# Down projection by seven products of quarters, with its sums on GpSimd and the next unit's first gate step placed among them

## Time and profile before

| | us |
|---|---|
| median of 3 runs | 4031.17 (4030.34 to 4031.83) |
| profiled execution | 4027.15 |
| its span | 4025.4 |
| feed-forward stage, first to last down product | 104 to 1058 |

### The profile page before, as it was taken

The page is one execution under the profiler, slowest core; times in us unless marked ns, Lnnn a source line. Parts: engine busy times, 40 slices in busy tenths (PEclk is TensorE's granted clock), DMA queues, the critical chain, the costliest instruction groups (busy, mean ns, idle before and its releaser), DMA issues. The chain is left out here.

```text
span 4025.4 us, 83987 instructions
## 1 busy us (share of the span) xinstructions
PE 3942.0 (98%) x29304; PEld 3015.1 (75%) x29304; DVE 3097.8 (77%) x6628; ACT 2298.9 (57%) x5920; POOL 1500.1 (37%) x1881
## 2 busy tenths in 40 slices
PE   7999999999999999999999999999999999999998
PEld 6788787887677777777777776777777777777775
DVE  6666666666588888888888887887888888887885
ACT  2222222222377777667677766767776767677674
POOL 2332232322233333333333334334444444444444
PEclk9999999999999999999999999999999999999999
DMA  4212111120443435344344454444444445445443
GB/s 151 49 37 50 25 50 38 38 50 19 146 113 96 102 100 132 98 104 103 104 106 102 106 143 127 107 132 119 123 115 122 116 120 131 132 116 134 121 109 97
DMA packets 813542, 400.79 MB, mean 100 GB/s; under 512 B 475584, under 2 KB 738752, under 8 KB 813120
## 3 DMA queue, kind: packets, MB, share of 16 engines
q1 hardware_dynamic: 777024, 340.17, 32.4%
q10 hardware_dynamic: 36096, 55.24, 5.0%
HBM read 242.57 MB, written 152.63 MB: 98 GB/s over the span
## 5 line engine op out<-in xcount | busy, mean ns | idle before, releaser
L1250 PE MATMUL bank<-xtile,wt 128*128 128x259 f32 x4096 | 1077.1, 391 | 6.5 <-PEq L766 2.5
L1250 PEld LDWEIGHTS bank<-xtile,wt 128*128 128x128 f32 x4096 | 727.2, 191 | 136.1 <-issue 43.7
L1732 ACT ACTIVATE xyinv<-bank 128x512 f16<-128x512 f32 x768 | 449.9, 590 | 222.0 <-PE bank L1675 217.9
L1989 PE MATMUL bank<-wot,xnt 128*128 128x512 f32 x1024 | 530.9, 610 | 4.0 <-DMA xnt<-x_scratch 3.2
L1708 DVE TENSOR_TENSOR wlev<-bank,mask 128x256 f16<-128x256 f32 x768 | 315.9, 415 | 164.1 <-PE bank L1675 161.1
L1379 DVE SCALAR_TENSOR_TENSOR vraw<-bank,taps,vraw 128x256 f32<-128x256 f32 x768 | 361.1, 476 | 33.8 <-ACT vraw L1372 19.9
L550 PE MATMUL bank<-hb,wt 128*128 128x128 f32 x2816 | 375.5, 277 | 8.3 <-DVE part L590 5.7
L550 PEld LDWEIGHTS bank<-hb,wt 128*128 128x128 f32 x2816 | 349.4, 194 | 17.6 <-issue 7.2
L1675 PEld LDWEIGHTS bank<-xyinv,lth 128*128 128x128 f16 x3584 | 202.6, 98 | 166.4 <-issue 88.3
L613 POOL TENSOR_TENSOR hid<-part 128x256 f32<-128x256 f32 x176 | 139.4, 792 | 473.3 <-ACT part L605 473.3
L1639 POOL TENSOR_TENSOR ltl<-ltm,lth 128x512 f16<-128x512 f32 x128 | 155.7, 1216 | 416.4 <-ACT lth L1633 416.4
(11 more groups left out here) (233 smaller groups left out, 8845.5 us busy)
## 6 DMA issues: line engine op xcount, KB each, us to landing
v_scratch<-vraw SPq DMA_DIRECT2D x64, 512.0 KB, 3.2
vtok<-v_scratch SPq DMA_DIRECT2D x512, 64.0 KB, 2.2
x_scratch<-tq SPq DMA_DIRECT2D x508, 64.0 KB, 1.8
xnt<-x_scratch SPq DMA_DIRECT2D x508, 64.0 KB, 2.5
grows<-row_scratch ACTq DMA_DIRECT2D x126, 256.0 KB, 3.7
k_scratch<-kraw SPq DMA_DIRECT2D x32, 512.0 KB, 2.7
ktok<-k_scratch SPq DMA_DIRECT2D x256, 64.0 KB, 2.1
b_scratch<-kraw SPq DMA_DIRECT2D x256, 64.0 KB, 1.8
```

Source lines behind the costliest of these rows:

```text
L1250: j = pe.matmul(b_p[:, 0:WIN], wt[:, k, c:c + P], xtile[:, par, k, :], **st)
L1732: act.activation(dst, b_inv[p][:].rearrange("p (a h b s) -> p a h b s", a=2, h=HEADS, s=z), ACT.Copy).then_inc(s[f"xy_sb{p}"], 1)
L1989: i = pe.matmul(b_o[:], xnt[:, h], wot[:, h], start=(h == 0), stop=(h == GV - 1))
```

## The change

The down projection becomes seven products too. Features 0 to 4 and 5 to 9 and the two halves of the 512 columns give the blocks d11, d12, d21, d22 of `w_down`; the same features and the two halves of the tokens give c11, c12, c21, c22 of `hid`. Feature block 10 is left over, and its four quarter products are added to four of the seven. POOL makes the weight sums e1, e2, e4 (new tiles) and e3 (in place of d12) once, in steps 0 to 2 (`pool_down_weights`, at "tokens" of unit 0, "stats" and "router" of unit 1). It makes the row sums r1 and r3 after each hid 5 to 9 (`pool_down_rows`), and r2, r4 and `last` in `pool_down`; r2 and r3 and r4 lie in place of c11, c21 and c12. The seven parts down 0 to 6 use 256 columns of banks 6 and 7. Bank 6 gathers sums over down 0, 2, 4, 5; ACT copies it after down 0, 2 and 4, times `routed` (`act_down`), POOL adds rows of h (`dsum`), and DVE selects four quarters (`dve_down`).

In `order`, down 0 and 1 stand where down 0 stood, down 2 to 6 where down 1 stood, and gate step 0 of the next unit is moved ahead of down 5. `dsum`, `last` and `wba` now lie in the end of `wt`, so the load of the z weights moves behind the last store. Some semaphores are merged; a negation of `neg_a` (L676) becomes part of another operation.

```diff
+        FH = FT // 2
+        DOWN = 7
+        lo, hi = slice(0, D // 2), slice(D // 2, D)
+        left, right = slice(0, P), slice(P, 2 * P)
+        d11, d12, d21, d22 = (wd_sb[:, i * FH:(i + 1) * FH, c] for i in range(2) for c in (lo, hi))
+        e3, (e1, e2, e4) = d12, (sb(f"wd_t{i}", [P, FH, D // 2]) for i in (1, 2, 4))
+        c11, c12, c21, c22 = (hid[:, i * FH:(i + 1) * FH, t] for t in (left, right) for i in range(2))
+        r1d, r2d, r3d, r4d = sb("down_s1", [P, FH, P]), c11, c21, c12
+        beyond = both[:, 2 * KT * FF:]
+        dsum = beyond[:, 0:3 * D // 2].rearrange("p (i c) -> p i c", i=3)
+        last = beyond[:, 3 * D // 2:3 * D // 2 + P]
+        DS_W, DS_U = 4, 17
+        DS_S1, DS_S3, DS_S2A, DS_S2, DS_A, DS_LAST, DS_S4, DS_U2, DS_U3 = 9, 10, 11, 12, 13, 14, 15, 16, 17
...
+        def pool_down_weights(pool, step):
+
+            if step == 0:
+                pool.wait_ge(s["d_in"], 16)
+                pool.tensor_tensor(e1[:], d12, d11, ALU.subtract).then_inc(s["dn_pool"], 1)
+                pool.wait_ge(s["dn_pool"], 1)
+                pool.tensor_tensor(e2[:], d22, e1[:], ALU.subtract).then_inc(s["dn_pool"], 1)
+            elif step == 1:
+                pool.wait_ge(s["dn_pool"], 2)
+                pool.tensor_tensor(e4[:], d21, e2[:], ALU.subtract).then_inc(s["dn_pool"], 1)
+            else:
+                pool.tensor_tensor(e3, d22, d12, ALU.subtract).then_inc(s["dn_pool"], 1)
+
+        def pool_down_rows(pool, u, f):
+
+            i = f - FH
+            pool.wait_ge(s["hid_sb"], FT * u + f + 1)
+            pool.tensor_tensor(r1d[:, i], c21[:, i], c22[:, i], ALU.add).then_inc(s["dn_pool"], 1)
+            pool.wait_ge(s["dn_pool"], DS_W + DS_U * u + 2 * i + 1)
+            pool.tensor_tensor(r3d[:, i], c11[:, i], c21[:, i], ALU.subtract).then_inc(s["dn_pool"], 1)
+
+        def pool_down(pool, u, i):
+
+            at, rows, take = DS_W + DS_U * u, h[:, u % 2], pool.tensor_tensor
+            if i == 0:
+                pool.wait_ge(s["d_ps"], DOWN * u + 1)
+                pool.wait_ge(s["dn_pool"], at + DS_S3)
+                for part_of in (slice(0, 2), slice(2, FH)):
+                    take(r2d[:, part_of], r1d[:, part_of], c11[:, part_of], ALU.subtract).then_inc(s["dn_pool"], 1)
+                pool.wait_ge(s["dn_act"], 3 * u + 1)
+                pool.wait_ge(s["hk"], 2 * NJ * (u + 1))
+                take(dsum[:, 0], dsum[:, 0], rows[:, 0, lo], ALU.add).then_inc(s["dn_pool"], 1)
+                pool.wait_ge(s["hid_sb"], FT * (u + 1))
+                take(last, hid[:, FT - 1, left], hid[:, FT - 1, right], ALU.subtract).then_inc(s["dn_pool"], 1)
+            elif i == 1:
+                pool.wait_ge(s["d_ps"], DOWN * u + 2)
+                pool.wait_ge(s["dn_pool"], at + DS_S2)
+                take(r4d, c12, r2d, ALU.subtract).then_inc(s["dn_pool"], 1)
+            elif i == 2:
+                pool.wait_ge(s["dn_act"], 3 * u + 2)
+                take(dsum[:, 1], dsum[:, 1], rows[:, 0, hi], ALU.add).then_inc(s["dn_pool"], 1)
+            elif i == 4:
+                pool.wait_ge(s["dn_act"], 3 * u + 3)
+                take(dsum[:, 2], dsum[:, 2], rows[:, 1, hi], ALU.add).then_inc(s["dn_pool"], 1)
+
+        def pe_down(pe, u, i):
+
+            at, sums = DS_W + DS_U * u, bank[6][:, lo]
+            outs, w10 = bank[7][:, lo], wd_sb[:, FT - 1]
+
+            def product(dst, rows, w, start, stop=True):
+                for f in range(FH):
+                    ins = pe.matmul(dst, rows[:, f], w[:, f], start=start and f == 0, stop=stop and f == FH - 1, skip_group_check=True)
+                return ins
+
+            if i == 0:
+                if u == 0:
+                    pe.wait_ge(s["d_in"], 16)
+                else:
+                    pe.wait_ge(s["selw"], 4 * u - 1)
                 pe.wait_ge(s["h_sb"], added(min(u + 2, UNITS_F)))
-            for f in range(FT):
-                if j == 0:
-                    pe.wait_ge(s["hid_sb"], FT * u + f + 1)
-                i = pe.matmul(bank[6 + j % 2][:], hid[:, f, j * P:(j + 1) * P], wd_sb[:, f, :], start=(f == 0), stop=(f == FT - 1))
-            i.then_inc(s["d_ps"], 1)
-
-        def dve_select(dve, u, j):
-            n = NJ * u + j
-            if n >= 2:
-                dve.wait_ge(s[f"g_out{j % 2}"], 16 * (n // 2))
-            dve.wait_ge(s["hk"], 2 * n + 2)
-            dve.wait_ge(s["d_ps"], n + 1)
-            dve.scalar_tensor_tensor(out=sel[:, j % 2, :], in0=bank[6 + j % 2][:], scalar=routed[:, u % 3, j:j + 1], in1=h[:, u % 2, j, :],
-                                     op0=ALU.mult, op1=ALU.add).then_inc(s["selw"], 1)
-
-        def act_select(act, u, j):
-            act.wait_ge(s["selw"], NJ * u + j + 1)
-            act.activation(sel[:, j % 2, :], sel[:, j % 2, :], ACT.Silu).then_inc(s["g_done"], 1)
+                pe.wait_ge(s["hid_sb"], FT * u + FH)
+                ins = product(sums, c11, d11, True)
+            elif i == 1:
+                if u:
+                    pe.wait_ge(s["selw"], 4 * u)
+                pe.wait_ge(s["hid_sb"], FT * u + 2 * FH)
+                product(outs, c12, d21, True, False)
+                pe.wait_ge(s["hid_sb"], FT * (u + 1))
+                ins = pe.matmul(outs, hid[:, FT - 1, left], w10[:, lo], start=False, stop=True, skip_group_check=True)
+            elif i == 2:
+                pe.wait_ge(s["dn_act"], 3 * u + 1)
+                pe.wait_ge(s["dn_pool"], at + DS_S2A)
+                for f in range(FH):
+                    if f == 2:
+                        pe.wait_ge(s["dn_pool"], at + DS_S2)
+                    ins = pe.matmul(sums, r2d[:, f], e2[:, f], start=False, stop=f == FH - 1, skip_group_check=True)
+            elif i == 3:
+                pe.wait_ge(s["selw"], 4 * u + 1)
+                product(outs, r1d, e1, True, False)
+                ins = pe.matmul(outs, hid[:, FT - 1, right], w10[:, hi], start=False, stop=True, skip_group_check=True)
+            elif i == 4:
+                pe.wait_ge(s["dn_act"], 3 * u + 2)
+                if u == 0:
+                    pe.wait_ge(s["dn_pool"], DS_W)
+                ins = product(sums, r3d, e3, False)
+            elif i == 5:
+                pe.wait_ge(s["dn_act"], 3 * u + 3)
+                product(sums, c22, e4, False, False)
+                ins = pe.matmul(sums, hid[:, FT - 1, right], w10[:, lo], start=False, stop=True, skip_group_check=True)
+            else:
+                pe.wait_ge(s["selw"], 4 * u + 2)
+                pe.wait_ge(s["dn_pool"], at + DS_S4)
+                product(outs, r4d, d22, False, False)
+                ins = pe.matmul(outs, last, w10[:, hi], start=False, stop=True, skip_group_check=True)
+            ins.then_inc(s["d_ps"], 1)
+
+        def act_down(act, u, i):
+
+            if i == 0 and u:
+                act.wait_ge(s["selw"], 4 * u)
+            act.wait_ge(s["d_ps"], DOWN * u + i + 1)
+            scale = routed[:, u % 3, i // 4:i // 4 + 1]
+            act.activation(dsum[:, i // 2], bank[6][:, lo], ACT.Identity, scale=scale).then_inc(s["dn_act"], 1)
+
+        def dve_down(dve, u, i):
+
+            at = DS_W + DS_U * u
+
+            def select(j, half, src, rest):
+                dve.scalar_tensor_tensor(out=sel[:, j, half], in0=src, scalar=routed[:, u % 3, j:j + 1], in1=rest, op0=ALU.mult, op1=ALU.add).then_inc(s["selw"], 1)
+
+            if i == 1:
+                if u:
+                    dve.wait_ge(s["g_out0"], 16 * u)
+                dve.wait_ge(s["dn_pool"], at + DS_A)
+                dve.wait_ge(s["d_ps"], DOWN * u + 2)
+                select(0, lo, bank[7][:, lo], dsum[:, 0])
+            elif i == 4:
+                if u:
+                    dve.wait_ge(s["g_out1"], 16 * u)
+                dve.wait_ge(s["dn_pool"], at + DS_U3)
+                dve.wait_ge(s["d_ps"], DOWN * u + 4)
+                select(1, hi, bank[7][:, lo], dsum[:, 2])
+            elif i == 5:
+                dve.wait_ge(s["hk"], 2 * NJ * (u + 1))
+                dve.wait_ge(s["d_ps"], DOWN * u + 6)
+                select(1, lo, bank[6][:, lo], h[:, u % 2, 1, lo])
+            elif i == 6:
+                dve.wait_ge(s["dn_pool"], at + DS_U2)
+                dve.wait_ge(s["d_ps"], DOWN * u + 7)
+                select(0, hi, bank[7][:, lo], dsum[:, 1])
+
+        def act_select(act, u, i):
+            act.wait_ge(s["selw"], 4 * u + i - 2)
+            act.activation(sel[:, 6 - i, :], sel[:, 6 - i, :], ACT.Silu).then_inc(s["g_done"], 1)
...
-            order.append((("down", 0), u - 1))
+            order += [(("down", i), u - 1) for i in range(2)]
             if u + 1 < UNITS_F:
                 order += [(("normalise",), u + 1), (("router",), u + 1)]
-            order.append((("down", 1), u - 1))
+            order += [(("down", i), u - 1) for i in range(2, DOWN)]
+        for u in range(1, UNITS_F):
+            order.remove((("gate", 0), u))
+            order.insert(order.index((("down", 5), u - 1)), (("gate", 0), u))
...
```

(61 more changed lines are left out.)

9 lines of the change are left out of this document (1 added, 8 removed).

## The result

| us | before | after |
|---|---|---|
| median (4 runs each) | 4031.44 (4030.34 to 4031.83) | 4151.98 (4142.79 to 4155.75) |
| profiled execution | 4027.15 | 4155.75 |
| its first attention product | 1060.35 | 1180.54 |

The ratio is 1.0293 (95% interval 1.0281 to 1.0304): slower by 120.5 us by the medians, forecast 112. The profiled executions differ by 128.6: 120.2 until the first attention product, 8.4 behind it. The one of after is the longest of its four.

What follows compares the result with a forecast made beforehand. PE was taken to bound the kernel, always busy in the feed-forward stage. -32.7 (products) + 91.7 + 10.2 + 2.1 + 0.9 (waits) + 38.5 (clock) + 1 (engines slowing each other) = +111.7, giving 4143 us; range 4096 to 4178.

Steps and rivals of the forecast that it cites:

- The products: PE's down projection: 78 records of 0.216 us replace 44 of 0.429, saving 2.04 us a unit, 32.7 over 16 units.
- The wait: Before down 2, PE waits 7.05 us for r2d, queued on POOL behind the variance step, in 14 of 16 units.
- behind the same keep steps: Remark in the rival that the saving arrives (4000 us, chance 0.03): down 3's select also stands behind DVE's keep steps.
- The clock: After each of 14 long waits PE returns at half rate, losing 2.75 us each, 38.5 in all.
- The rival without the clock: PE waits before down 2 but returns at 2.4 GHz: sum +73.2, 4104 us, chance 0.13.
- The sign given for it: Granted clock goes to 0.50 after each long wait; mean clock of the span falls from 0.994 to about 0.985.
- 1 us for the whole, bounds 0 and 4: Cost of POOL and DVE slowing each other while POOL makes the four weight sums (2.9 us each) at the start.
- The last unit but one: Without the variance step there, down 3 waits for DVE's select and starts at t = 9.0, not 6.91: 2.1 us.
- Against: DVE is idle in just that stretch: Argument against port contention: DVE stands idle while POOL makes r2d and dsum.
- a rival (4158): Port contention: r2d and dsum at 1.45 times their price add 15 us in all, 4158 us, chance 0.09.
- The loads: The z weights' 2 MB load leaves after the last g store, around 1060: taken as 0, upper bound 5 us.
- The moved gate step: Before down 5, it covers ACT's second copy of bank 6, which would otherwise cost PE 0.86 us.

Runs made afterwards that it cites:

- e3: No run: a weight sum POOL makes. The experiment moving e3 and e4 behind down 2's work of the first unit, on the rewritten list: 4004.4 us, ratio 0.9926.
- the rewritten list: Changed kernel with all engines' order rewritten, softplus, keep and statistics steps going between the down parts: 3998.24 us, ratio 0.9925 against the kernel before.
- the first experiment: Changed kernel with only POOL's variance of the next-but-one unit moved behind its work for down 1: 4136.6 us, ratio 1.0266 against the kernel before.
- the one with unused products: Changed kernel with 16 unread products of 256 columns on PE ahead of down 2 in 14 units: 4122.79 us, ratio 1.0229 against the kernel before.
- the one with POOL held back: Changed kernel where, in the last unit but one, POOL's down work waits until DVE has done its softplus parts: one execution, 4152.87 us.

## Why the prediction was right, and where its sizes were off

Slower was right, by the mechanism named and in its range. Profile against profile, by stretches of the sum:

| part | forecast | measured |
|---|---|---|
| start until the first down product | +1 | +5.5 |
| first unit | +10.9 | +11.2 |
| 13 units | 13 x 7.76 = +100.9 | 13 x 7.58 = +98.5 |
| last unit but one | +0.1 | +5.9 |
| last unit | -1.1 | -1.0 |
| attention stage | 0 | +8.4 |

**The products.** -2.04 a unit was exact, as the rewritten list shows where nothing hides it.

**The wait.** 7.05 forecast, 7.27 measured, both from t = 4.75, where down 1 ends by the pace of its records (the waits list counts from the modelled end of the last record and has 7.10). The 0.2 is DVE, slowed in its softplus parts beside POOL's row sums. That it is the list and not POOL's price is shown by taking the operations out of the way (ratio 0.9925). That moving POOL's variance alone would not do is a second thing that the forecast had only as a remark (down 3's select "behind the same keep steps").

**The clock.** 2.75 forecast. From unit to unit down 2 to 6, with the moved gate step among them, take 15.65, 16.6 or 17.1 us in turn instead of 14.03: 1.6 to 3.1, mean 2.4. Keeping PE busy gives 2.28 back. The rival without the clock (4104) is out. That one earlier gap of 5.6 us gave a figure so near the mean is partly luck, as the price differs by a factor of two from wait to wait. The sign given for it, a mean clock near 0.985, was missed: it is 0.977. The granted clock falls while PE still waits (0.74 over 400.20 to 407.20), and so in the feed-forward stage it is at half for 146.8 us, 17.1 before; what of it lies in the wait costs nothing. The Trainium skill, TensorE: Matmul & The Clock Gate, section HAM oscillation, says that a wait which returns in each tile sends the engine to half rate each time; the traces agree, 14 waits of 14, and after the wait of 6.41 us in the first experiment too (4.63 for ten products).

**The start: the term that failed.** "1 us for the whole, bounds 0 and 4" was +5.5, beyond the bound. The step counted only the 5.6 us gap that lay under the sums and took the slowing from POOL's L286. It is DVE that is slowed, and PE waits for DVE here. DVE and POOL of after at that place, and DVE of before, where the same L330 is L316:

```profile
60.91 3.55 DVE L330 TENSOR_SCALAR xn<-xn,mv,rstd 128x512 f32<-128x512 f32 x2 [1.16 <-POOL rstd L283]
```

```profile
60.85 2.88 POOL L638 TENSOR_TENSOR wd_t<-wd_sb,wd_t 128x1280 f32<-128x1280 f32 x1
```

```profile
61.01 1.00 DVE L316 TENSOR_SCALAR xn<-xn,mv,rstd 128x512 f32<-128x512 f32 x2 [1.15 <-POOL rstd L269]
```

DVE loses 2.5 us at once, and PE has its fourth gate step 2.5 us later; after, then before:

```profile
66.74 1.22 PE L564 MATMUL bank<-hb,wt 128*128 128x128 f32 x4 [8.69 <-DVE part L604]
```

```profile
64.29 1.22 PE L550 MATMUL bank<-hb,wt 128*128 128x128 f32 x4 [5.73 <-DVE part L590]
```

At 71.24 the next sum does it again to L811, 3.94 where it was 2.19, and the small products behind it come 4.2 us late (79.35 against 75.15) and at half rate. That these sums are the cause is shown by the experiment that moves e3 and e4 away: the first down product is back at 103.90.

**The last unit but one.** Here the forecast had down 3 2.1 us late; it waited 5.52 and came back at half rate. Without the variance in its way POOL starts r2d at once, and its five operations in a row run beside DVE's L811: 4.84 for 1.78, 3.1 of the 3.6 us by which the select is late. The half rate of down 3 (4.63 for 2.32) is the other 2.3. "Against: DVE is idle in just that stretch" holds for the 14 units with the long wait, up to down 3 (behind it the pair L330 takes 2.16 beside POOL's L666, at 409.25, for which nobody on PE waits); it was never asked of this unit. As a rival (4158) contention is out: r2d took 1.68 for two operations, dsum 0.72, their list price.

**The loads, ACT and the gate step.** The late z load costs nothing, as taken. The moved gate step pays 0.83 a unit, forecast 0.86.

**The attention stage** is 8.4 longer, but that is not shown to be the change. Over all profiles it takes 2955 to 2973 us, with 24 to 47 us of it at half rate: 27.3 in the one of before and 46.9 in that of after (half of the difference is 9.8 us, enough for the 8.4), 41.0 in the second profile of the changed kernel, which is 3.3 us shorter. The kernel before with the late load took 2963.1, with 35.8. Why an execution has more or less of it stays open, and chance alone is not shown either: the four profiles with the changed kernel's list and its waits in place (this one, its second, the one with unused products and the one with POOL held back) have 2970.1 to 2973.4, the six with the rewritten list 2954.9 to 2968.0. The changed kernel's own runs spread too (mean clock 0.977 for 4155.75, 0.980 for 4142.79).

## What to carry to other kernels

When a product is split into chained parts on several engines, ask of each new input what stands ahead of it in its maker's queue, not what making it costs: 17 more operations of POOL a unit were free in the middle units of the rewritten list, and one old wait in front of them cost 7 us, plus 2.3 for the clock. Take all waits that lie over each other away together, here by the order of the list; one alone gained 0.3%. Work put on POOL is free only where DVE, while POOL works, is not what the bounding engine waits for.

## What the hardware did that I had not expected

Beside POOL operations of two inputs, some of DVE's operations on SBUF nearly stop, while POOL keeps its pace. The two L330 began 0.06 us after POOL's 2.88 us L638 and ended 0.73 after its end, so they did little of their 1.00 beside it. The seven L811 in the last unit but one still needed 1.38 us after POOL's L666 had ended at 1106.95. Taken one by one, the first four end 0.08 us behind the ends of POOL's operations (at 1104.36, 1105.04, 1105.46 and 1106.95), as if each were held until POOL's had ended. DVE's L614, which reads PSUM and only one tile of SBUF, took its 0.56 beside the same kind of POOL operation (at 71.79). In the experiment with POOL held back DVE's first L539 was under way when POOL started; there POOL was stretched too, 2.34 for 1.69.

The Trainium skill, page SBUF — State Buffer, section Who interferes with whom, describes this: an exclusive lock on a shared port pair, for DVE instructions with two SBUF inputs or in a two-port mode, the second one blocked until the first ends. The traces agree: the 0.08 us above fit a full block, and the 0.73 nearly does, where one would leave 1.00. Weighed in the forecast, it would have asked which DVE operations stand beside the sums.

PE kept its clock over 2.7 us without work, as over the 1.38 us above, but lost it behind the 2.48 us of the experiment with POOL held back, and in the kernel before behind a gap of 1.76 us at 75.15 (the granted clock is 0.50 from 76.56 to 79.97). So the length of a wait alone does not tell. One wait of 4.12 us cost half rate for a whole down part, and the price of the same 7 us wait goes round in three steps, 1.6, 2.6 and 3.1 us.
